# Inverse root of the layer norms in 11 links instead of 17, and the second norm one step later, in a gated cross-attention and mixture-of-experts kernel

## The reference

```python
x = x + tanh(g_xattn) * xattn(layernorm(x), ctx)      # 16 heads, latent keys and values, softmax
x = x + tanh(g_ffn) * ffn(layernorm(x))               # 8 routed experts (2 per token) + a shared MLP

def layernorm(x, eps=1e-5):
    m, v = mean(x), var(x)                            # over the 512 features of a token
    return (x - m) / sqrt(v + eps)
```

## Time and profile before

| | us |
|---|---|
| median of 3 runs | 2048.73 (2046.67 to 2054.72) |
| profiled execution | 2055.81 |
| its span, first to last instruction | 2054.0 |
| PE busy | 1925.0 (94%) |
| DVE busy | 913.0 (44%) |
| POOL busy | 715.7 (35%) |
| ACT busy | 666.8 (32%) |

### The profile page before, as it was taken

One profiled execution on the slowest core, in us unless ns is written; L12 is line 12 of the kernel. 1 busy time (PEld: TensorE's weight loads), 2 busy tenths in 40 slices (PEclk: granted clock), 3 DMA queues, 4 the chain that ended last, 5 costly groups with the idle time before them and its releaser, 6 DMA issues.

```text
span 2054.0 us, 32243 instructions
## 1 busy us (share of the span) xinstructions
PE 1925.0 (94%) x11801; PEld 1071.0 (52%) x11972; DVE 913.0 (44%) x1819; ACT 666.8 (32%) x1905; POOL 715.7 (35%) x779
## 2 busy tenths in 40 slices
PE   7698989898989899889999999999999999999999
PEld 7455555555555555444445555555554444444444
DVE  5665555555555555436633222222223424243243
ACT  5555555555555555522011222222210000000000
POOL 5655555555555555610022343343302110110101
PEclk9999999999999999999999999999999999999999
DMA  9444554544444555351237999889953621321202
GB/s 295 110 93 102 100 104 98 105 98 103 100 101 101 108 126 116 96 129 56 84 79 156 229 250 218 218 214 223 211 117 116 126 78 36 87 82 26 77 16 87
DMA packets 427300, 250.01 MB, mean 122 GB/s; under 512 B 360368, under 2 KB 366256, under 8 KB 427184
## 3 DMA queue, kind: packets, MB, share of 16 engines
q1 hardware_dynamic: 415664, 210.61, 44.4%
q0 software_dynamic: 11520, 37.76, 6.4%
HBM read 113.02 MB, written 48.23 MB: 79 GB/s over the span
## 4 chain that ended last, share of the span: by engine, by line
PE 57%; DVE 14%; issue 12%; ACT 8%; POOL 7%; DMA 1%; SPq 1%; DVEq 0%; POOLq 0%; ACTq 0%
PE score L726 11%; PE o L811 7%; PE score L800 7%; PE o L737 5%; PE p_bank L726 5%; PE m_bank L726 5%; ACT arena L888 4%; PE p_bank L800 3%; PE m_bank L800 3%; DVE arena L1011 3%; PE c_bank L737 3%; PE t_bank L737 3%; POOL arena L1380 3%; DVE arena L1081 2%; POOL arena L1375 2%
## 5 line engine op out<-in xcount | busy, mean ns | idle before, releaser
L584 PE MATMUL o<-arena 128*128 128x512 bf16 x1473 | 342.3, 382 | 6.6 <-DVE arena L1011 1.7
L888 ACT ACTIVATE arena<-score,arena 128x128 f32<-128x128 f32 x512 | 181.5, 367 | 291.6 <-DVE arena L1081 291.6
L633 PE MATMUL p_bank<-arena 128*128 128x256 bf16 x1536 | 198.0, 290 | 40.7 <-DVE arena L1011 40.7
L584 PEld LDWEIGHTS o<-arena 128*128 128x128 bf16 x1536 | 151.8, 100 | 160.2 <-issue 5.8
L726 PE MATMUL score<-arena 128*128 128x512 bf16 x1036 | 233.7, 379 | 1.1
L1375 POOL TENSOR_TENSOR arena<-arena 128x512 bf16<-128x512 f32 x128 | 149.8, 1171 | 234.6 <-ACT arena L841 233.6
L633 PEld LDWEIGHTS p_bank<-arena 128*128 128x128 bf16 x1536 | 154.2, 104 | 73.4 <-DVE arena L1011 43.5
L726 PEld LDWEIGHTS score<-arena 128*128 128x128 bf16 x1056 | 103.3, 98 | 124.4
L1466 POOL TENSOR_TENSOR arena<-arena 128x1088 bf16<-128x1088 f32 x32 | 71.9, 2247 | 274.5 <-ACT arena L918 274.5
L811 PE MATMUL o<-arena 128*128 128x512 bf16 (+1 forms) x681 | 160.1, 379 | 2.0
L1011 DVE TENSOR_TENSOR arena<-arena 128x512 bf16<-128x512 f32 (+2 forms) x219 | 152.2, 705 | 19.9 <-ACT arena L910 5.6
(11 more groups left out here) (164 smaller groups left out, 2792.9 us busy)
## 6 DMA issues: line engine op xcount, KB each, us to landing
xrow_d<-arena SPq DMA_DIRECT2D x80, 256.0 KB
arena<-w_expert SPq DMA_DIRECT2D x32, 544.0 KB, 5.3
arena<-w_shared SPq DMA_DIRECT2D x22, 384.0 KB, 3.4
arena<-x SPq DMA_DIRECT2D x16, 512.0 KB, 4.9
arena<-x SPq DMA_DIRECT2D x32, 256.0 KB, 2.8
x_d<-arena SPq DMA_DIRECT2D x32, 256.0 KB, 2.4
xn_d<-arena SPq DMA_DIRECT2D x32, 256.0 KB, 2.2
arena<-x_d SPq DMA_DIRECT2D x8, 1024.0 KB
```

Of the source, the lines that this page charges most:

```text
L584: mm = pe.matmul(o_bank[b % 2][:, :], lhsT=cT[u % 2][:, a, h, :], rhs=M_w[:, w, head_of(hg, h), :], start=(hg == 0 and n == 0), stop=(hg = ...
L633: mm = pe.matmul(o, lhsT=B_w[:, a, t, cols], rhs=xT1[g % 2][:, w, t, :], start=(n == 0), stop=(n == 3 * KT - 1))
L888: mm = act.activation(prob[:, u % 4, h, :], score_bank[u % 2][:, h * S:(h + 1) * S], ACT.Exp, bias=neg_max[:, u % 4, h:h + 1], accum_out=d ...
```

## The change

It touches DVE's program only. Links 1 to 3 become BN_AGGR, one for each column, which gives mean and variance, and an addition of eps. The integer guess stays. The three Newton steps become one step of third order and one Newton step. Two constants move into later links. Of the 11 links, the last five stand together behind step 1's projection subtraction. `norms` is split in two: `norm_1` stays behind the last link in step 1, `norm_2` goes to the end of step 2, behind the two subtractions of norm 1. The waits for the statistics move ahead of the reciprocal of step 0.

```diff
--- before.py
+++ after.py
@@ -25,7 +25,7 @@
 NG = NB // 2
 EPS = 1e-5
 RSQRT_SEED = float(0x5F3759DF)
-RSQRT_OPS = 17
+RSQRT_OPS = 11
 
 E = 8
 I = 352
@@ -141,8 +141,7 @@
         xT32 = words(2 * D).rearrange("p (b n) -> p b n", b=2)
         xn2_rows = [halves(words(D)).rearrange("p (l n) -> p l n", l=2) for _ in range(2)]
         stats = words(4 * 6).rearrange("p (c n) -> p c n", c=4)
-        mean = words(4)
-        mean_dif = words(4)
+        mean_var = words(8).rearrange("p (c n) -> p c n", c=4)
         var_eps = words(4)
         shifted = words(4)
         rstd = words(4)
@@ -1021,11 +1020,16 @@
                         for i in which:
                             rsqrt_link(i, g2, g1, it)
 
+                if m == 0:
+                    if within(g2, NG):
+                        wait(dve, stat2, 2 * g2 + 2, 4, it)
+                    if within(g1, NG):
+                        wait(dve, stat1, 2 * g1 + 2, 4, it)
                 u = k + 5
                 if within(u, NU):
                     wait(dve, exped, u + 1, 16, it)
                     dve.reciprocal(rden[:, u % 4, :], den[:, u % 4, :]).then_inc(inverted, 1)
-                links(*((1, 2) if m == 0 else (10, 11)))
+                links(*((1,) if m == 0 else ()))
                 if k % 4 == 3 and within(k // 4, NB):
                     b = k // 4
                     wait(dve, o_mm, b + 1, 4, it)
@@ -1041,11 +1045,9 @@
                     wait(dve, ct_hi, u + 1, 16, it)
                     lower(cT[u % 2][:, LO].rearrange("p h n -> p (h n)"), ctx_bank[u % 2][:, :],
                           cT[u % 2][:, HI].rearrange("p h n -> p (h n)")).then_inc(ct_lo, 1)
-                links(*((3, 4) if m == 0 else (12, 13)))
+                links(*((2, 3) if m == 0 else (6,)))
                 if k % 2 == 0:
                     row_max(k + 6, it)
-                links(*((5,) if m == 0 else (14,)))
-                links(*((6, 7) if m == 0 else (15, 16)))
                 q = k + 12
                 if within(q, 8 * NG):
                     wait(dve, pr_hi, q + 1, 16, it)
@@ -1058,9 +1060,11 @@
                     for s in range(2):
                         wait(dve, xn1_hi, 2 * (c + 2) + s + 1, 4, it)
                         lower(xn1_rows[s][:, LO, :], x_ln[:, s, :], xn1_rows[s][:, HI, :]).then_inc(xn1_lo, 1)
-                links(*((8, 9) if m == 0 else (17,)))
+                links(*((4, 5) if m == 0 else (7, 8, 9, 10, 11)))
                 if m == 1:
-                    norms(g2, g1, it)
+                    norm_1(g1, it)
+                if m == 2:
+                    norm_2(g2, g1, it)
                 if -12 <= k < -4:
                     for h in (2 * (k + 12), 2 * (k + 12) + 1):
                         dve.wait_ge(m_hi, h + 1)
@@ -1086,55 +1090,50 @@
                 has2, has1 = within(g2, NG), within(g1, NG)
                 cols = slice(0 if has2 else 2, 4 if has1 else 2)
                 v, y, n = var_eps[:, cols], rstd[:, cols], newton[:, cols]
-
-                m_e, m_o, q_e, q_o = (stats[:, cols, f] for f in (1, 4, 2, 5))
-                mu, dif = mean[:, cols], mean_dif[:, cols]
                 if i == 1:
-                    if has2:
-                        wait(dve, stat2, 2 * g2 + 2, 4, it)
-                    if has1:
-                        wait(dve, stat1, 2 * g1 + 2, 4, it)
-                    dve.tensor_tensor(mu, m_e, m_o, ALU.add)
-                    dve.tensor_tensor(dif, m_e, m_o, ALU.subtract)
-                    dve.tensor_tensor(v, q_e, q_o, ALU.add).then_inc(rsqrt_step, 1)
+                    for j in range(cols.start, cols.stop):
+                        ins = dve.bn_aggr(mean_var[:, j, :], stats[:, j, :])
+                    ins.then_inc(rsqrt_step, 1)
                     return
                 wait(dve, rsqrt_step, RSQRT_OPS * g1 + i - 1, 2 * RSQRT_OPS, it)
                 if i == 2:
-                    dve.tensor_scalar(mu, mu, 0.5, None, ALU.mult)
-                    dve.tensor_tensor(dif, dif, dif, ALU.mult)
-                    ins = dve.tensor_scalar(v, v, 1.0 / D, EPS, ALU.mult, ALU.add)
+                    ins = dve.tensor_scalar(v, mean_var[:, cols, 1], EPS, None, ALU.add)
                 elif i == 3:
-                    ins = dve.scalar_tensor_tensor(out=v, in0=dif, scalar=0.25, in1=v, op0=ALU.mult, op1=ALU.add)
-                elif i == 4:
                     ins = dve.tensor_scalar(shifted[:, cols].bitcast(I32), v.bitcast(I32), 1, None,
                                             ALU.arith_shift_right)
-                elif i == 5:
+                elif i == 4:
                     ins = dve.tensor_scalar(y.bitcast(I32), shifted[:, cols].bitcast(I32), -1.0, RSQRT_SEED,
                                             ALU.mult, ALU.add)
-                elif i % 4 == 2:
+                elif i in (5, 9):
                     ins = dve.tensor_tensor(n, v, y, ALU.mult)
-                elif i % 4 == 3:
+                elif i == 6:
                     ins = dve.tensor_tensor(n, n, y, ALU.mult)
-                elif i % 4 == 0:
-                    ins = dve.tensor_scalar(n, n, -0.5, 1.5, ALU.mult, ALU.add)
+                elif i == 7:
+                    ins = dve.scalar_tensor_tensor(out=n, in0=n, scalar=-10.0 / 3.0, in1=n, op0=ALU.add, op1=ALU.mult)
+                elif i == 8:
+                    ins = dve.scalar_tensor_tensor(out=y, in0=n, scalar=5.0, in1=y, op0=ALU.add, op1=ALU.mult)
+                elif i == 10:
+                    ins = dve.scalar_tensor_tensor(out=n, in0=n, scalar=-0.5 * 0.375 ** 3, in1=y,
+                                                   op0=ALU.mult, op1=ALU.mult)
                 else:
-                    ins = dve.tensor_tensor(y, y, n, ALU.mult)
+                    ins = dve.scalar_tensor_tensor(out=y, in0=n, scalar=1.5 * 0.375, in1=y,
+                                                   op0=ALU.add, op1=ALU.mult)
                 ins.then_inc(rsqrt_step, 1)
 
-            def norms(g2, g1, it):
-
-                if within(g2, NG) or within(g1, NG):
+            def norm_1(g1, it):
+                if within(g1, NG):
                     wait(dve, rsqrt_step, RSQRT_OPS * (g1 + 1), 2 * RSQRT_OPS, it)
-                if within(g1, NG):
                     for s in range(2):
-                        dve.tensor_scalar(x_ln[:, s, :], x_ln[:, s, :], mean[:, 2 + s:3 + s],
+                        dve.tensor_scalar(x_ln[:, s, :], x_ln[:, s, :], mean_var[:, 2 + s, 0:1],
                                           rstd[:, 2 + s:3 + s], ALU.subtract, ALU.mult).then_inc(xn1_ready, 1)
+            def norm_2(g2, g1, it):
                 if within(g2, NG):
+                    wait(dve, rsqrt_step, RSQRT_OPS * (g1 + 1), 2 * RSQRT_OPS, it)
                     for s in range(2):
                         b = 2 * g2 + s
                         wait(dve, xn2_lo, b - 1, 4, it)
                         wait(dve, l2_mm, b - 1, 4, it)
-                        dve.tensor_scalar(xn2[:, s, :], x1[b % 4], mean[:, s:s + 1], rstd[:, s:s + 1],
+                        dve.tensor_scalar(xn2[:, s, :], x1[b % 4], mean_var[:, s, 0:1], rstd[:, s:s + 1],
                                           ALU.subtract, ALU.mult).then_inc(xn2_ready, 1)
 
             def lower_a(half):
```

## The result

| | before | after |
|---|---|---|
| median (lowest to highest), 4 runs each | 2047.7 (2046.16 to 2054.72) | 2062.76 (2057.71 to 2063.7) |
| ratio, 95% interval | | 1.0062 (1.0033 to 1.009) |
| span of the profiled execution | 2054.0 | 2055.9 |
| DVE busy | 913.0 | 873.0 |
| PE busy | 1925.0 | 1935.7 |

The kernel became slower, as forecast, but by 13 to 15 us and not by 28: 2062.8 instead of 2077. DVE has 40 us less work, and nothing of it is gained. The two profiled spans are nearer to each other than the medians, since the profiled execution of before (2055.81) is slower than any of its runs in the table, and the one of after is its fastest (2057.71).

What follows compares the result with a forecast made beforehand. PE leads the attention stage, with a second slackless chain through ACT, POOL and DVE from step 4. Later transposes (+0.4) and a clock fall (+2.5) make the period +2.25, total +28: 2084 profiled, median 2077, range 2060 to 2100 us.

Steps and rivals of the forecast that it cites:

- The gains in steps 0 and 1: DVE in steps 0 and 1: 0.9, 1.1 and 1.0 us gained, 3.0 a period.
- P: Start of DVE's projection subtraction in step 2, predicted to come 3.0 us earlier.
- my bounds: DVE in step 0: each BN_AGGR between 0.07 and 0.68 us; 0.9 gained at 0.07 to 0.12, lost at 0.68.
- the sum: Period 50.55 + 0.4 + 2.5 = 53.45 us against 51.2, +2.25; +29 over thirteen periods, total +28.
- norm_2's hold: DVE in step 2: POOL's waiting share subtraction goes first, so norm_2 runs from P+2.9 to P+3.9.
- N: End of norm_2 and start of step 3's reciprocal, predicted at P+3.9.
- The slip-in rival: Step 2: norm_2 gets SBUF before POOL's waiting operation, N at P+2.8, clock holds; -19, 2030 us; chance 0.20.
- SP's queue: Transposes queue behind loads awaiting norm_2: 4 us PE gap before step 4's c_bank; L633 at P+10.9, 0.4 later than before.
- The clock: PE in step 4: a clock fall in every period hits L633, on the chain, for +2.5 us.
- The ends: Periods outside c = 1 to 13: c = 0 gains about 1.5 us, c = 14 to 16 nothing.
- The range: 2060 to 2100 us: norm_2 ahead of POOL takes 14 off, BN_AGGR at its upper bound puts 23 on.

Runs made afterwards that it cites:

- the repeat: The changed kernel measured once more, nothing altered: 2063.88 us, ratio 1.0065 to the kernel before.
- run 5: Changed kernel with norm_2 ahead of step 2's two norm-1 subtractions, still behind the projection subtraction: 2021.22 us, ratio 0.9851 to the kernel before.
- run 4: Changed kernel with SP's two loads of x issued in step 4 instead of step 2: 2040.08 us, ratio 0.9943 to the kernel before.

## Why the prediction was right in direction and wrong in size

**The gains in steps 0 and 1: right.** From step 7's residual update to P the changed kernel takes 21.98 (401.33 to 423.31) where it took 25.09: 3.1 earlier, 3.0 predicted. Four BN_AGGR lasted 0.35, near the low end of my bounds. Between context subtraction and next reciprocal it is 3.96, 4.0 predicted. The last four links are 0.19 to 0.20 apart, each behind a semaphore, the 0.2 of the sum; the rule drawn from the Trainium skill (VectorE: DVE Perf Modes, The DRAIN you can't avoid), a semaphore for nothing, does not hold for this chain of small operations.

**norm_2's hold: right here.** Its first operation took 1.38 of the 1.84, because POOL got in between; N is P+3.65, 3.9 predicted, in eleven of the thirteen periods. In the last two, with POOL's L1437 ahead as well, it is P+5.03, and L632 of step 4 starts at P+12.2: two times 1.1 us that the prediction had not seen. The slip-in rival fell for this order, though run 5 shows that the turn goes the other way in another.

**SP's queue: right.** c_bank at P+8.45 (8.1 predicted) with a gap of 4.28 (about 4), step 4's L632 at P+11.1 (10.9 predicted). Run 4 confirms the cause. The period without a clock term should have been 50.95; the usual periods take 51.2 to 51.9 with 0.2 to 0.4 of a longer L632 in them.

**The clock: the step that failed.** "It hits L633 of step 4, on the chain: +2.5" (now L632). The fall came in every period, as predicted, but earlier than in the case that I took its price from. There, in the earlier trace rows, the gap ended right at L633 and the low clock lay over it. Here it begins as the gap ends (0.95 in 431 to 432 us, then 0.50), so it first lengthens c_bank (1.37 for 0.82) and the scores (1.46 for 0.84). These two only fill the time until xT1 has landed, which PE would have waited for. The period at 380 us shows it: there c_bank still ran at full clock, L632 waited for the DMA, and it started at P+11.03, no earlier than the P+11.0 to P+11.2 of the periods in which both were slow:

```profile
379.90 0.82 PE L596 MATMUL c_bank<-arena 128*128 128x512 bf16 x3 [4.04 <-DMA arena<-arena]
380.66 1.46 PE L610 MATMUL score<-arena 64*128 64x128 bf16 x24
382.73 3.44 PE L632 MATMUL p_bank<-arena 128*128 128x256 bf16 x24 [0.61 <-DMA arena<-arena]
```

By 436 the clock is back, and L632 takes 3.19, not 5.3. It takes 2.96 to 3.19 in five periods in a row, 3.4 to 4.6 in the others but one (2.78). So the term of the sum that was wrong is the +2.5 for the clock on L633. L632 is 0.7 longer than at full clock on average here, 1.2 in the repeat. A fall must be priced by what it lies over: 1.6 in run 4, where nothing fills its place, 0.2 to 0.4 in the usual period here.

**Late landings, not in the sum.** In three of the thirteen periods here (220, 274 and 688 us), and in five of the repeat's, one of the two xT1 transposes lands 4.6 to 5.2 behind its issue where it usually takes 3.1 to 3.7, and L632 starts 1.0 to 1.7 later than in the other periods, whatever the clock does: at 692 it then ran at full clock (2.78), at 278 it took 4.61, and that period, from scores to scores, was 55.0. With these, the period is 1.3 us above 50.95 here and 2.1 in the repeat, where the sum had 2.5. Against the mean period of before it is 0.8 and 1.6 longer, for a forecast of 2.25.

**The ends: undersized.** I gave c = 0 a gain of 1.5 and c = 14 to 16 nothing. The scores of step 4 in c = 0 start 4.1 earlier (121.76 for 125.85), and the period up to c = 14, with norm 2 but no xT1 of a next group, is 3.2 shorter. That is 5.8 us less than forecast. The span was to grow by 28 and grew by 1.9: the ends are 5.8 of the difference, the shorter period 13 x (2.25 - 0.8) = 19. In the repeat the span grew by 8.0: the ends are 7.9 of the 20 that are missing (c = 0 is 6.3 earlier there), the period 13 x (2.25 - 1.6) = 8, and the rest lies behind the attention stage, which ends 11.5 later than before's. Between the medians only 14 are missing, because the profiled execution of before is 7 above its median.

**The range.** 2062.8 lies in the range of 2060 to 2100, but by luck: its lower end stood for norm_2 let in ahead of POOL, which did not happen.

**What stays open.** Why the fall begins with c_bank in most periods and behind it in some, and how long it lasts; why xT1 lands late in some periods; with both, why executions of the changed kernel differ by up to 15 us; how the 49 us of norm_2's place divide between POOL's turn and SP's queue, since run 4 removes the queue (23 us) but leaves a gap and its fall, and run 5 changes both.

## What to carry to other kernels

Ask of every added or moved vector operation where its engine waits anyway. Behind a row maximum, with an exponential and a cast to wait for, 17 links and both norms take 1988 us. With 11 links, five of them and norm 1 behind step 1's last subtraction, it is 2014 with norm_2 there too, and 2063 with norm_2 at the end of step 2. When an operation moves later, look for the queue whose head waits for it: here two loads that nobody needed soon held up three transposes that everybody did. And a stall can take a clock fall along: it did in about half of the cases behind 2.71 us of idling in the kernel before, in twelve of thirteen behind 3.6 or more in run 4, and in all thirteen behind 3.7 or more in the changed kernel. What the fall costs depends on whether the work beneath it had slack.

## What was not expected of the hardware

- The turn between POOL and DVE. In the changed kernel POOL came up at 424.91, during the second of norm 1's subtractions, and got in when that ended, ahead of norm_2. In run 5 it came up at 556.50, during the first of the same two, and waited 1.1 through both. So POOL's turn comes at the end of the running operation in one case and one later in the other. Whether it hangs on the waits that the next DVE operation carries was not tried.
- A DVE operation on 128 x 4 int32 (L1102) took 0.65 in step 0, to the end of a rope operation of POOL (408.06 + 0.72), where the same kind took 0.16 later in the step (L1105): the hold is not a matter of float types.
- The same transposes, two a period, landed 3.2 to 3.7 us behind their issue in most periods and one of them 4.6 to 4.9 in three of thirteen (up to 5.2 in five of the repeat's), with the same issues of SP ahead of them.
